# Mixture-of-experts tail of a one-core decoder kernel: fp16 two-part products, a transposed first layer, biases as products, and one row load a tile

## The reference, cut to what matters

```python
x = x + ffn(layernorm(x))           # 8192 tokens of 128 numbers
# ffn: 8 experts, D = 128, FF = 512
logits = x @ router_W + router_b;  probs = softmax(logits);  top1 = argmax(probs)
h = relu(x @ W1[e] + b1[e])          # 128 -> 512
y = h @ W2[e] + b2[e]                # 512 -> 128
out = probs[e] * y                   # e = top1 of the token
```

## Time and profile before

| what | value |
|---|---|
| median of three runs | 1951.23 us (1947.08 to 1954.17) |
| span of the profiled execution | 1942.5 us |
| time of the profiled execution itself | not given beside the three; its span is 8.7 us under their median |
| last stage, from its first TensorE work | 1559.4 us to the end |
| scatter to `sorted_x` on POOL | 1647.3 to 1728.7 us |
| tiles on TensorE | 1732.0 to 1933.5 us |
| last transpose of `X` (L1291) | ends near 1605 us |
| the two weight loads on SP (L1226, L1227) | issued in 3.4 and 1.9 us; other issues on SP take 0.3 to 0.43 us |
| mean granted TensorE clock | 0.821 |

### The profile page before, as it was taken

One profiled execution on the slowest core, in us unless ns is written; L12 is line 12 of the kernel. 1 busy time (PEld: TensorE's weight loads), 2 busy tenths in 40 slices (PEclk: granted clock), 3 DMA queues, 4 the chain that ended last, 5 costly groups with the idle time before them and its releaser, 6 DMA issues. The chain is left out here.

```text
span 1942.5 us, 82660 instructions
## 1 busy us (share of the span) xinstructions
PE 1543.4 (79%) x34335; PEld 1369.0 (70%) x34336; DVE 1169.9 (60%) x4397; ACT 759.4 (39%) x1849; POOL 207.1 (11%) x427
## 2 busy tenths in 40 slices
PE   1557777777536999999999999999999965029997
PEld 0356666666416999999999999999989854016665
DVE  5878888888793555555555555555555566014444
ACT  2455666566472333333333333333333311013332
POOL 0000000000001000000000000000000000753333
PEclk9778888888856788888898788888897755569999
DMA  6000000000114000000000000000000070222221
GB/s 206 1 2 0 0 0 0 0 0 0 50 37 199 0 0 0 0 0 0 0 0 0 0 0 0 0 0 0 0 0 0 1 228 6 103 86 71 71 72 50
DMA packets 42813, 57.39 MB, mean 30 GB/s; under 512 B 5754, under 2 KB 32892, under 8 KB 40856
## 3 DMA queue, kind: packets, MB, share of 16 engines
q1 hardware_dynamic: 36672, 42.90, 7.2%
q0 software_dynamic: 5376, 12.66, 1.9%
q10 hardware_dynamic: 728, 1.34, 0.2%
HBM read 30.52 MB, written 26.88 MB: 30 GB/s over the span
## 5 line engine op out<-in xcount | busy, mean ns | idle before, releaser
L1512 DVE TENSOR_TENSOR hb<-psH,b_sb 128x512 f32<-128x512 f32 x72 | 49.8, 692 | 168.7 <-issue 88.9
L858 PE MATMUL z_a<-h_a,WL 128*128 128x64 f16 x2304 | 137.4, 219 | 5.9 <-DVE h_a L1045 1.9
L858 PE MATMUL z_b<-h_b,WL 128*128 128x64 f16 x2304 | 131.0, 214 | 7.2 <-issue 2.9
L895 PE MATMUL sc_a<-h_a,KH 128*128 128x16 f16 x4096 | 124.7, 171 | 2.5 <-DVE h_a L1053 2.5
L858 PEld LDWEIGHTS z_a<-h_a,WL 128*128 128x128 f16 x2304 | 112.6, 115 | 14.2 <-DVE h_a L1053 7.7
L895 PE MATMUL sc_b<-h_b,KH 128*128 128x16 f16 x4096 | 122.4, 170 | 0.0
L935 PEld LDWEIGHTS mx_a<-pmv_a,VH 128*128 128x128 f16 x4096 | 109.8, 97 | 11.2 <-DVE pmv_a L1081 11.0
L895 PEld LDWEIGHTS sc_a<-h_a,KH 128*128 128x128 f16 x4096 | 115.4, 98 | 2.7 <-DVE h_a L1053 2.6
L935 PE MATMUL mx_a<-pmv_a,VH 128*128 128x16 f16 x4096 | 114.4, 170 | 3.5 <-DVE pmv_a L1081 0.3
L858 PEld LDWEIGHTS z_b<-h_b,WL 128*128 128x128 f16 x2304 | 107.4, 112 | 13.6 <-DVE h_b L1053 6.7
L935 PEld LDWEIGHTS mx_b<-pmv_b,VH 128*128 128x128 f16 x4096 | 108.4, 96 | 11.6 <-DVE pmv_b L1081 11.1
(11 more groups left out here) (282 smaller groups left out, 3849.5 us busy)
## 6 DMA issues: line engine op xcount, KB each, us to landing
sorted_x<-zt SPq DMA_DIRECT2D x9, 1032.0 KB, 11.9
xr<-sorted_x SPq DMA_DIRECT2D x72, 65.0 KB
xg<-sorted_x SPq DMA_DIRECT2D x72, 64.0 KB
XT<-in_ctxT SPq DMA_DIRECT2D x1, 4096.0 KB, 13.0
x_scratch<-X SPq DMA_DIRECT2D x1, 4096.0 KB, 15.9
TOK<-x_scratch SPq DMA_DIRECT2D x4, 1024.0 KB, 10.3
w_sb<-in_w SPq DMA_DIRECT2D x1, 2048.0 KB, 12.8
b_sb<-in_b SPq DMA_DIRECT2D x1, 2048.0 KB, 20.0
```

The lines of the kernel that those rows point to most:

```text
L858: mm = nc.tensor.matmul(q.z[layer][:, j * GB:(j + 1) * GB], WL[:, blk + j, w, :], mov[m], start=False, stop=False, skip_group_check=True)
L895: mm = nc.tensor.matmul(A.S[:, WIDE * n:WIDE * (n + 1)], KH[:, k, pair * P:(pair + 1) * P], A.h[1][:, 2 * n:2 * n + WIDE // 2, :].rearrang ...
L1512: nc.vector.tensor_tensor(hb[:, u, :], psH[:, u, :], b1_sb[:, bass.ds(col, FF)], ALU.add).then_inc(v_hb, 1)
```

## The change

The expert weights are loaded as float32 into the space of `X`, which is free by then, and are split into an fp16 high part and an fp16 low part (`w1h`, `w2h`, both scaled by powers of two found at run time). The tokens and the hidden layer are split in the same way (`xh`, `hh`): ACT writes the high part, VectorE the low part. Each 128 x 128 product becomes three fp16 products (high by high, high by low, low by high).

The first layer is computed transposed: the weight block is stationary and the tokens move, so the hidden layer comes out with its features on the partitions and the four transposes of a tile go. Both biases become one bf16 product each: `BB` holds three parts of the scaled biases, `pick` a matrix that selects the expert's rows. VectorE no longer adds biases, and no longer loads a column.

A tile's whole rows come with one DMA into a ring of eight (`xg`), and the ring is freed when the tile's store has landed. TensorE's order in a step is now: column load and output of tile i, column load and hidden of i+2, turn of i+4. The loop does eight steps a turn; eight steps before it and four after it are straight code.

The diff, cut to its core (the unchanged scatter, the router and the allocation of small tiles are left out; of the lines that go only the tiles stand here, since the functions of the kernel before are printed above; the lines are moved left by twelve columns):

```diff
-w1_sb = sb("w1_sb", [P, NE * FF])
-w2_sb = sb("w2_sb", [P, NE * FC * D])
-b1_sb = sb("b1_sb", [P, NE * FF])
-b2_sb = sb("b2_sb", [P, NE * D])
+W1F, W2F = X[:, 0:NE * FF], X[:, NE * FF:]
+w1h = sb("w1h", [P, 2, NE * FF], F16)
+w2h = sb("w2h", [P, 2, NE * FF], F16)
+pick = sb("pick", [P, NE * FC, P], BF16)
+pickf = pick[:, :, :].rearrange("p n t -> p (n t)")
...
-xg = sb("xg", [P, 2, D])
-xr = sb("xr", [P, 4, ROW - AT_X2])
+RING = 8
+SX = 16.0
+xg = sb("xg", [P, RING, ROW])
+xh = sb("xh5", [P, 2, 2, P], F16)
+hh = sb("hh", [P, 2, 2, FF], F16)
+gate5 = sb("gate5", [P, RING])
+ys = sb("ys", [P, RING, D])
...
 def run_tiles(eng, step):
+    for i in range(-4, 4):
+        step(i, i % RING)
+    with eng.Fori(4, NT - 4 - RING + 1, RING) as i:
+        for k in range(RING):
+            step(i + k, (4 + k) % RING)
+    for i in range(NT - 4, NT):
+        step(i, i % RING)
+def run_ring(eng, step):
+    for j in range(RING):
+        step(j, j)
+    with eng.Fori(RING, NT - RING + 1, RING) as j:
+        for k in range(RING):
+            step(j + k, k)
...
+        sync.wait_ge(g_bz, 1)
+        for k in range(3):
+            sync.dma_start(bb[32 * k:32 * k + 32, 0, :], b1.rearrange("e (c f) -> (e c) f", c=FC)).then_inc(s_b5, 16)
+            for e in range(NE):
+                r = 32 * k + FC * e
+                sync.dma_start(bb[r:r + 1, 1, :], b2[e:e + 1, :]).then_inc(s_b5, 16)
+        sync.wait_ge(p_a, NCH)
+        sync.dma_start(W1F.rearrange("p (e f) -> p e f", e=NE), w1.rearrange("e p f -> p e f")).then_inc(s_w5, 16)
+        sync.dma_start(W2F.rearrange("p (e c n) -> p e c n", e=NE, c=FC),
+                       w2.rearrange("e (c p) n -> p e c n", p=P)).then_inc(s_w5, 16)
+        def load(j, r):
+            wait(sync, d_ys[r], 2 * (j - r))
+            sync.dma_start(xg[:, r, :], x_rows[:, bass.ds(j, 1), :].rearrange("p j d -> p (j d)")).then_inc(d_x[r], 16)
         sync.wait_ge(d_sc, 16 * T)
+        run_ring(sync, load)
+        for r in range(RING):
+            sync.wait_ge(d_ys[r], 2 * NT)
...
+        pool.memset(bb[:, :, :], 0.0).then_inc(g_bz, 1)
+        pool.wait_ge(v_id, 1)
+        pool.tensor_copy(pick[:, :, :], id3[:, :].unsqueeze(2).broadcast_to([P, NE * FC, P])).then_inc(g_pick, 1)
...
+        pe.wait_ge(v_mx5, 4)
+        nc.tensor.transpose(psY[0:4, 0, 0:P], mx4[:, :], ident[:, :]).then_inc(p_sc5, 1)
+        pe.wait_ge(v_sc5, 2)
+        nc.tensor.matmul(psY[:, 1, 0:4], ones[0:4, :], dg[:, :], start=True, stop=True).then_inc(p_sc5, 1)
+        def column(j):
             return pe.value_load(etab[0:1, 0, bass.ds(j, 1)], min_val=0, max_val=(NE - 1) * FF)
+        def turn(j, u, r):
+            pe.wait_ge(d_x[r], 2 * (j - r) + 16)
+            wait(pe, v_xl, j - 1)
+            nc.tensor.transpose(psX[:, u, 0:P], xg[:, r, 0:D], ident[:, :]).then_inc(p_xt, 1)
         def hidden(j, u, col):
+            pe.wait_ge(v_xl, j + 1)
+            wait(pe, v_hl, j - 1)
+            nc.tensor.matmul(psH[:, u, :], BB[:, 0, :], pickf[:, bass.ds(col, FF)], start=True, stop=False,
+                             skip_group_check=True)
             for c in range(FC):
+                w = [w1h[:, k, bass.ds(col + c * P, P)] for k in range(2)]
+                for a, b in ((0, 0), (0, 1), (1, 0)):
+                    mm = nc.tensor.matmul(psH[:, u, c * P:(c + 1) * P], w[a], xh[:, u, b, :],
+                                          start=False, stop=False, skip_group_check=True)
+            mm.then_inc(p_h, 1)
         def output(j, u, col):
+            pe.wait_ge(v_hl, j + 1)
+            wait(pe, v_ys, j - 1)
+            nc.tensor.matmul(psY[:, u, 0:P], pickf[:, bass.ds(col, P)], BB[:, 1, :], start=True, stop=False,
+                             skip_group_check=True)
             for c in range(FC):
+                w = [w2h[:, k, bass.ds(col + c * P, P)] for k in range(2)]
+                for a, b in ((0, 0), (0, 1), (1, 0)):
+                    mm = nc.tensor.matmul(psY[:, u, 0:P], hh[:, u, a, c * P:(c + 1) * P], w[b],
+                                          start=False, stop=False, skip_group_check=True)
             mm.then_inc(p_y, 1)
         pe.wait_ge(v_slot, 2)
+        pe.wait_ge(v_bb, 1)
+        pe.wait_ge(v_wl, 2)
+        pe.wait_ge(g_pick, 1)
+        def step(i, r):
+            u = r % 2
+            if tile(i):
+                output(i, u, column(i))
+            if tile(i + 2):
+                hidden(i + 2, u, column(i + 2))
+            if tile(i + 4):
+                turn(i + 4, u, (r + 4) % RING)
         run_tiles(pe, step)
...
+        act.wait_ge(v_scale5, 1)
+        nc.scalar.activation(w1h[:, 0, :], W1F, ACT.Copy, scale=sw[:, S1:S1 + 1]).then_inc(a_wh, 1)
+        nc.scalar.activation(w2h[:, 0, :], W2F, ACT.Copy, scale=sw[:, S2:S2 + 1]).then_inc(a_wh, 1)
         def turned(j, u):
             act.wait_ge(p_xt, j + 1)
             wait(act, p_h, j - 1)
+            nc.scalar.activation(xh[:, u, 0, :], psX[:, u, 0:P], ACT.Copy, scale=SX).then_inc(a_xt, 1)
         def relu(j, u):
+            act.wait_ge(p_h, j + 1)
             wait(act, p_y, j - 1)
+            nc.scalar.activation(hh[:, u, 0, :], psH[:, u, :], ACT.Relu).then_inc(a_hh, 1)
+        def step(i, r):
+            u = r % 2
+            if tile(i + 2):
+                relu(i + 2, u)
+            if tile(i + 4):
+                turned(i + 4, u)
         run_tiles(act, step)
...
+        dve.wait_ge(s_b5, 16 * 3 * (1 + NE))
+        for q in range(2):
+            nc.vector.tensor_reduce(mx4[:, 2 * q + 1:2 * q + 2], bb[:, q, :], AX.X, ALU.max,
+                                    apply_absolute_value=True).then_inc(v_mx5, 1)
...
+        for q, w in enumerate((W1F, W2F)):
+            nc.vector.tensor_reduce(mx4[:, 2 * q:2 * q + 1], w, AX.X, ALU.max,
+                                    apply_absolute_value=True).then_inc(v_mx5, 1)
...
+        bwf, bhf, BBf = (t[:, :, :].rearrange("p a n -> p (a n)") for t in (bw, bhi, BB))
+        for part in range(3):
+            step(nc.vector.tensor_copy(bhf, bwf))
+            if part == 0:
+                step(nc.vector.tensor_scalar(BBf, bhf, rowk[:, 0:1], None, ALU.mult))
+            else:
+                step(nc.vector.scalar_tensor_tensor(BBf, bhf, rowk[:, part:part + 1], BBf, ALU.mult, ALU.add))
+            step(nc.vector.tensor_tensor(bwf, bwf, bhf, ALU.subtract))
+        nc.vector.sem_inc(v_bb, 1)
+        dve.wait_ge(v_scale5, 1)
+        dve.wait_ge(a_wh, 1)
+        nc.vector.scalar_tensor_tensor(w1h[:, 1, :], W1F, sw[:, S1:S1 + 1], w1h[:, 0, :],
+                                       ALU.mult, ALU.subtract).then_inc(v_wl, 1)
+        dve.wait_ge(a_wh, 2)
+        nc.vector.scalar_tensor_tensor(w2h[:, 1, :], W2F, sw[:, S2:S2 + 1], w2h[:, 0, :],
+                                       ALU.mult, ALU.subtract).then_inc(v_wl, 1)
+        def gate(j, r):
+            dve.wait_ge(d_x[r], 2 * (j - r) + 16)
+            nc.vector.tensor_scalar(gate5[:, r:r + 1], xg[:, r, AT_GATE:AT_GATE + 1], sw[:, UN:UN + 1], None,
+                                    ALU.mult).then_inc(v_gs, 1)
+        def finish(j, u, r):
             dve.wait_ge(p_y, j + 1)
+            dve.wait_ge(v_gs, j + 1)
+            nc.vector.scalar_tensor_tensor(ys[:, r, :], psY[:, u, 0:P], gate5[:, r:r + 1], xg[:, r, AT_X2:AT_GATE],
+                                           ALU.mult, ALU.add).then_inc(v_ys, 1)
+        def hidden_low(j, u):
+            dve.wait_ge(a_hh, j + 1)
+            nc.vector.scalar_tensor_tensor(hh[:, u, 1, :], psH[:, u, :], 0.0, hh[:, u, 0, :],
+                                           ALU.max, ALU.subtract).then_inc(v_hl, 1)
+        def turned_low(j, u):
+            dve.wait_ge(a_xt, j + 1)
+            nc.vector.scalar_tensor_tensor(xh[:, u, 1, :], psX[:, u, 0:P], SX, xh[:, u, 0, :],
+                                           ALU.mult, ALU.subtract).then_inc(v_xl, 1)
+        def tile_step(i, r):
+            u = r % 2
+            if tile(i):
+                finish(i, u, r)
+            if tile(i + 2):
+                hidden_low(i + 2, u)
+            if tile(i + 4):
+                turned_low(i + 4, u)
+                gate(i + 4, (r + 4) % RING)
         run_tiles(dve, tile_step)
```

More of the change, by code:

```diff
@@ L1185, in decoder_kernel @@
             d_sc = sem("d_sc")
-            d_xg = [sem(f"d_xg{u}") for u in range(2)]
+            s_w5 = sem("s_w5")
+            s_b5 = sem("s_b5")
+            g_bz = sem("g_bz")
+            v_id = sem("v_id")
+            g_pick = sem("g_pick")
+            v_mx5 = sem("v_mx5")
+            p_sc5 = sem("p_sc5")
+            v_sc5 = sem("v_sc5")
+            v_scale5 = sem("v_scale5")
+            a_wh = sem("a_wh")
+            v_wl = sem("v_wl")
+            v_bb = sem("v_bb5")
+            d_x = [sem(f"d_x{r}") for r in range(RING)]
             p_xt = sem("p_xt5")
             a_xt = sem("a_xt5")
+            v_xl = sem("v_xl5")
             p_h = sem("p_h")
-            v_hb = sem("v_hb")
-            p_ht = sem("p_ht")
```

(19 more changed lines are left out.)

127 lines of the change are left out of this document (30 added, 97 removed).

## The result

The changed kernel takes **2057.73 us** (median of 4 runs, 2055.35 to 2061.25), the kernel before 1949.38 in the runs beside it: a ratio of 1.055, 95% interval 1.0528 to 1.0571. Forecast were 2050, range 1985 to 2130. The profiled execution of after has a span of 2053.6 us against 1942.5: 111.1 us more.

What follows compares the result with a forecast made beforehand. The prediction took TensorE's instruction stream as the bound, ahead of its products in the loop. Products +101 us and last store -1 made 1951.2 + 100, near 2050 us; range 1985 to 2075, up to 2130 with every product's address computed anew.

Steps and rivals of the forecast that it cites:

- The bound: TensorE's instruction stream sets each tile: 18 register operations at 0.13 us and two column loads, 4.20 us a loop tile.
- Rival A: On TensorE, products bound the tile or the stream runs ahead, if an address costs under 0.02 us; middle 1910; chance 0.08.
- for about half: Sign expected in the tiles: TensorE busy for about half the time, its idle time put down to "issue".
- The tiles' sum: From the first transpose on, the products of all tiles end at 2034.5 instead of 1933.5 us, so +101.
- the last store: At the end of the tiles, the final store no longer queues behind another, -1 us.
- The preparation hidden behind the scatters: Before the tiles, weight splitting fits behind 81 us of scatters; scatters slowed by VectorE cost 0 to 5 us, taken as none.
- The 8.7 us: Whole kernel: the profiled span lies 8.7 us under the median of the runs, so the time is 1951.2 + 100.
- Rival C: TensorE idles over half a tile, its clock falls from 2.4 to 1.2 GHz: 0 to 0.3 us a tile; chance 0.1.
- B: In TensorE's tiles every product computes its address anew, 26 instead of 18, +75 us: 2125; chance 0.12.
- D: The change doesn't reach the path at all: product and stream lengths cancel, 1951; chance 0.02.
- the sum was 2.56: TensorE's stream a loop tile if addresses cost nothing: loads 1.28, waits 0.35, index and branch 0.23, 26 products at 0.027.
- the 0.23 that the prediction took for index and branch: In TensorE's loop, index arithmetic and branch take 0.23 us a tile of the earlier 0.36, branching every eight tiles.

## Why the prediction was right, point by point

- **The bound.** Right: the stream sets the tile, before and after. The count of 18 register operations, the reuse of an address by the products that share it, two loads, "issue" as the idle time: all as forecast. An address costs 0.12 to 0.125 us in three measurements, against 0.13 taken from the earlier trace rows. Rival A's point of decision lay at 0.02. One sign was off: TensorE was to be busy "for about half", and is for 27.89 of 40 us, 0.70. I had left out that the addresses stand between the products of a layer and stretch its busy time with them, from 0.67 to 1.00 us and more for twelve.
- **The tiles' sum.** +101 forecast for the products and -1 for the last store; +101.1 measured from first transpose to last store. The agreement is better than its parts. The loop tile is 4.21 us as forecast, but with a load at 0.74 instead of 0.64 (+0.20) and 18 addresses at 0.12 to 0.125 instead of 0.13 (-0.1 to -0.2): two errors that cancel, and that is luck.
- **The preparation hidden behind the scatters.** Here a step failed: "0 to 5 us for some 25 of them. I take none." It was 7.1 us, outside my own bounds, and in two scatters, not 25. I had bounded the effect by the 1.16 us of the first scatter, and asked whether VectorE's work fits into the scatters' time, not whether it holds them up. The two reductions over 4096 columns before them, 8.73 us together, and the other passes up to 256 columns wide left the scatters beside them at 0.96 to 1.15. The Trainium skill has the rule, which I did not weigh (SBUF — State Buffer, Who interferes with whom): a VectorE instruction with two SBUF inputs contends with a GpSimd instruction that reads SBUF, one in a two-port mode with any, and whoever comes second waits for the other's whole instruction; a reduction never does. The rows agree for the two-input passes of 4096 columns (4.86 and 4.09 us) and for the reductions. Whether the one-source pass (0.57 ns a column) ran in a two-port mode no row tells; its scatter (4.51 us) was not let in between the two passes. The same section infers that `tensor_tensor`, which takes only the shared read interface, leaves descriptor generation alone; the `scalar_tensor_tensor` here, with two SBUF inputs as well, did hold the indirect DMA, and the measurement decides. The pieces of 512 fit less well, since both sides only stretched a little, to 1.02 and 0.74 us. Why, these runs leave open.
- **The 7.7 us between 2050 and 2057.7** are nearly all this term: with it the sum is 2057. By the medians the change costs 2057.73 - 1949.38 = 108.4 us, and the tiles and the scatters together 101.1 + 7.1 = 108.2, closer than the interval of the ratio, some 4 us either way, can vouch for. The 8.7 us that I added between span and time are no constant: the changed kernel's profiled span is 4.1 us under its median. They cancel, since both ends of my sum carry them.
- **Rival C** came true in part, and of its 0 to 0.3 us a tile the lower end was right: the clock fell to about 0.83 in the tiles, and to 0.50 in the run with half the columns, at the same 4.21 us. **B** (26 addresses) did not come, nor did A and D.

## What to carry to other kernels

Count a matmul's dynamic address as an instruction of its own: in this program about 0.12 us of the sequencer for each distinct one and 0.64 to 0.74 us for each value loaded into a register, whatever the size of the product that uses it. Splitting float32 products into fp16 parts made the array's work shorter here and the addresses 3.6 times as many, and the stream decided. A list of waits names the event that came last; ask the code whether it is the one that was needed. When one engine's work is to hide behind another's, ask not only whether it is short enough, but whether a single long instruction can hold the other up; cutting it into pieces may be all that is needed.

## What had not been expected of the hardware

- A VectorE pass that reads and writes 4096 columns stops an indirect DMA's issue on POOL for its whole length, with two sources at 1.09 ns a column (4.86 and 4.09 us) as with one at 0.57 ns (4.51 us over two passes). A reduction over as many columns does not (0.96 us). Cut into 512 columns the pass raises a scatter from 0.96 to 1.02 us only.
- Loads and waits of a stream overlap with dispatch more than a sum of their spacings says: 2.01 us a tile where the sum was 2.56. The price of an address, in contrast, adds up.
- The written-out code of 76 steps ran no slower than the loop: 3.22 us a tile against 255.8 / 71 = 3.60 in the loop. 18 more loads in the loop, at 0.74 us each, are 0.19 of the 0.38; the rest fits the 0.23 that the prediction took for index and branch.
